# A linear-attention kernel: state carried on every 64 tokens instead of every 128

## What is computed

```python
qp, kp, v = phi(proj(Wq, bq)), phi(proj(Wk, bk)), proj(Wv, bv)   # phi = elu + 1
def step(carry, inp):
    kv, ksum = carry
    kt, vt, qt = inp
    kv = kv + einsum('bhd,bhe->bhde', kt, vt)
    ksum = ksum + kt
    num = einsum('bhd,bhde->bhe', qt, kv)
    den = einsum('bhd,bhd->bh', qt, ksum)[..., None] + EPS
    return (kv, ksum), num / den
...
x = x + out @ Wo.T + bo
```

## Time and profile before

| | |
|---|---|
| runs | 1939.35 us median of 3 (1937.93 to 1939.39) |
| profiled execution | 1939.27 us, span 1937.6 us |
| PE busy | 1904.0 us, 98% |
| VectorE busy | 1586.2 us, 82% |
| ScalarE busy | 664.3 us, 34% |
| POOL busy | 891.4 us, 46% |
| mean granted clock of PE | 0.997 |

### The profile page before, as it was taken

The page is one execution under the profiler, slowest core; times in us unless marked ns, Lnnn a source line. Parts: engine busy times, 40 slices in busy tenths (PEclk is TensorE's granted clock), DMA queues, the critical chain, the costliest instruction groups (busy, mean ns, idle before and its releaser), DMA issues. The chain is left out here.

```text
span 1937.6 us, 60626 instructions
## 1 busy us (share of the span) xinstructions
PE 1904.0 (98%) x25412; PEld 1671.4 (86%) x25412; DVE 1586.2 (82%) x3379; ACT 664.3 (34%) x1297; POOL 891.4 (46%) x979
## 2 busy tenths in 40 slices
PE   7999999999999999999999999999999999999997
PEld 6788888888888888888888888888888888888886
DVE  6878878887879888778878987887788897878787
ACT  4333333333333233333333333333332333323331
POOL 4355443455443554534554445545345544355422
PEclk9999999999999999999999999999999999999998
DMA  6343234433343432333423334323433334333222
GB/s 202 94 133 106 92 111 125 127 110 104 100 127 110 128 118 74 127 121 115 122 99 105 116 111 138 113 85 111 132 116 116 98 96 129 113 126 119 75 72 84
DMA packets 171202, 218.03 MB, mean 113 GB/s; under 512 B 24369, under 2 KB 85809, under 8 KB 170929
## 3 DMA queue, kind: packets, MB, share of 16 engines
q1 hardware_dynamic: 168528, 213.59, 34.7%
q10 hardware_dynamic: 2400, 0.55, 0.1%
HBM read 151.02 MB, written 63.04 MB: 110 GB/s over the span
## 5 line engine op out<-in xcount | busy, mean ns | idle before, releaser
L1258 POOL TENSOR_TENSOR k_sum<-k_sum,q_raw 128x512 f32<-128x512 f32 x128 | 165.0, 1290 | 556.2 <-DVE q_raw L933 556.2
L836 ACT ACTIVATE e_tmp<-ring,bias_n 128x512 f32<-128x512 f32 x256 | 176.1, 688 | 509.9 <-PE ring L651 506.8
L922 DVE TENSOR_TENSOR s_mask<-ring,causal 128x512 f32<-128x512 f32 x512 | 314.9, 678 | 0.0
L669 PE MATMUL ring<-wv_hi,xt_hi 128*128 128x260 f32 x1024 | 299.3, 292 | 0.0
L669 PE MATMUL ring<-wo_hi,o_hi 128*128 128x260 f32 x1024 | 287.8, 282 | 1.2 <-ACT o_hi L886 1.0
L669 PE MATMUL ring<-wv_lo,xt_hi 128*128 128x260 f32 x1024 | 288.8, 282 | 0.0
L669 PE MATMUL ring<-wv_hi,xt_lo 128*128 128x260 f32 x1024 | 288.8, 282 | 0.0
L669 PE MATMUL ring<-wo_lo,o_hi 128*128 128x260 f32 x1024 | 288.4, 282 | 0.0
L669 PE MATMUL ring<-wo_hi,o_lo 128*128 128x260 f32 x1024 | 287.3, 284 | 0.9 <-DVE o_lo L1170 0.9
L886 ACT ACTIVATE o_hi<-num_ps 128x512 fp32r<-128x512 f32 x128 | 76.4, 597 | 475.0 <-PE num_ps L750 474.9
L651 PE MATMUL ring<-xt_hi,wk_hi 128*128 128x512 f32 x512 | 207.9, 406 | 5.2 <-DVE xt_lo L998 3.2
(11 more groups left out here) (140 smaller groups left out, 4060.3 us busy)
## 6 DMA issues: line engine op xcount, KB each, us to landing
x_tok<-in_x SPq DMA_DIRECT2D x128, 256.0 KB, 3.7
res<-in_x SPq DMA_DIRECT2D x128, 256.0 KB, 2.8
out<-res SPq DMA_DIRECT2D x128, 256.0 KB, 2.1
x_in<-in_x_t SPq DMA_DIRECT2D x124, 256.0 KB, 4.6
keys_turned<-k_turned SPq DMA_DIRECT2D x112, 256.0 KB, 2.0
k_tok<-keys_turned SPq DMA_DIRECT2D x448, 64.0 KB, 2.0
x_rows<-moments_rows SPq DMA_DIRECT2D x31, 512.0 KB, 3.7
k_t<-in_wk_t SPq DMA_DIRECT2D x4, 256.0 KB, 8.3
```

What stands on the lines that cost most here:

```text
L669: mm = pe.matmul(bank[:, 0:HW], rows[a](k), w[b][:, k, h, :], start=n == 0, stop=n == 3 * KD - 1)
L836: act.activation(e_tmp[:, m], bank, ACT.Relu, bias=bias_n[:, m, g:g + 1], scale=-1.0).then_inc(phi_relu.handle, 1)
L922: dve.tensor_tensor(s_mask[:, j], ring[:, st.bank(u)].rearrange("p (g t) -> p g t", g=KD), repeat(causal, KD), ALU.mult).then_inc(free[st. ...
L1258: pool.tensor_tensor(k_sum[:, g], k_sum[:, g], q_raw[:, g], ALU.mult).then_inc(prod.handle, 1)
```

## The change

The unit of the carried state becomes 64 tokens (`HT = 64`), two halves s = 0 and 1 of a tile:

- The scores are formed only inside a half: for every head two products of 64 keys by 64 queries, on array tiles of 32 rows by 64 columns. 32 products instead of 16; a mask covers 256 elements per partition instead of 512.
- `from_tile` has 32 products, each over 64 keys and 64 queries, on array tiles of 64 rows by 32 columns. Products whose rows lie on one side of the array and whose place in `num` belongs to the other bank ("crossed" ones, half of them) go to a place of their own, `apart`. ScalarE copies `apart` to SBUF (`apart_kept`), and VectorE adds it into `num` (`join_halves`) before `o_hi`.
- `from_state` and `add_state` are called for each half: the early half (`early_half`, s = 0) of the next tile directly behind the output projection of this tile, the late half (`late_half`, s = 1) where the whole visit stood. For s = 0 too, VectorE sums the state (`sum_state`, behind the residual) and ScalarE keeps it (`keep_state`, at the top of the tile), before the late half can read it. Each half of the state has its own `kv_ps`.
- The last tile of a pair now needs keys as well, for its early half. In the last step keys are turned, sent and fetched a tile earlier.
- Two small constants more are set at the start.

The diff, cut to its core:

```diff
+HT = P // 2
-    KEY_TILES = [(b, c) for b in range(n_blocks) for c in range(TPB) if b % 2 == 0 or c < TPB - 1]
+    KEY_TILES = [(b, c) for b in range(n_blocks) for c in range(TPB)]
-    s_mask = sb("s_mask", [P, HPG, KD, P])
+    s_mask = sb("s_mask", [P, HPG, KD, HT])
-    causal = sb("causal", [P, P])
+    causal = sb("causal", [P, HT])
+    apart_kept = sb("apart_kept", [P, 2, P])
-    kv_ps = num_ps[:, 0, 2 * P:2 * P + KD * HD]
+    kv_ps = [num_ps[:, n, 2 * P:2 * P + KD * HD] for n in range(2)]
+    apart = num_ps[:, :, 3 * P:4 * P]
...
             for g in range(KD):
...
-                for j, u in enumerate(scores_of(c)):
-                    rows = slice(j * HD, (j + 1) * HD)
-                    mm = pe.matmul(ring[:, st.bank(u), g * P:(g + 1) * P], k_t[rows, par, g, t], q_div[rows, par, g, t],
-                                   start=True, stop=True, skip_group_check=True, tile_position=(j * HD, 0))
+                for s in range(2):
+                    t = slice(c * P + s * HT, c * P + (s + 1) * HT)
+                    for j, u in enumerate(scores_of(c)):
+                        rows = slice(j * HD, (j + 1) * HD)
+                        mm = pe.matmul(ring[s * HT:(s + 1) * HT, st.bank(u), g * HT:(g + 1) * HT],
+                                       k_t[rows, par, g, t], q_div[rows, par, g, t], start=True, stop=True,
+                                       skip_group_check=True, tile_position=(j * HD, s * HT))
...
+        def from_state(off, c, s):
+
+            n = kv_before(off, c, s)
+            if first_of_pair(off, c, s):
                 return
+            pe.wait_ge(kv_kept.handle, kv_kept.at(HPG * n))
+            begins = (0, 1) if s == 0 else (1,) if first_of_pair(off, c, 0) else ()
             for g, j in HEADS_OF_PASSES:
+                r = j // 2
+                rows, t = slice(r * HT, (r + 1) * HT), slice(c * P + s * HT, c * P + (s + 1) * HT)
+                out, col = num_at(g, j, s)
+                pe.matmul(out, kv_diag[rows, g, j * HD:(j + 1) * HD], q_div[rows, off % 2, g, t],
+                          start=r in begins and g < 2, stop=r != s, skip_group_check=True, tile_position=(r * HT, col))
+
+        def add_state(off, c, s):
+
+            if last_of_pair(off, c, s):
+                return
+            n = KEY_TILES.index((off, c))
+            pe.wait_ge(keys_in[n % 2].handle, 16 * HPG * (n // 2 + 1))
+            rows = slice(s * HT, (s + 1) * HT)
+            for g in range(KD):
+                for j in range(HPG):
+                    cols = slice((g * HPG + j) * HD, (g * HPG + j + 1) * HD)
+                    mm = pe.matmul(kv_ps[s][j * HD:(j + 1) * HD, g * HD:(g + 1) * HD], k_tok[rows, n % 2, j, g],
+                                   v_tok[rows, c, cols], start=first_of_pair(off, c, s) and g == 0, stop=True,
+                                   skip_group_check=True, tile_position=(s * HT, j * HD))
+            if s == 0:
+                mm.then_inc(kv_added.handle, 1)
...
+            for four in range(0, HEADS, HPG):
+                for s in range(2):
+                    rows = slice(s * HT, (s + 1) * HT)
+                    for g, j in HEADS_OF_PASSES[four:four + HPG]:
+                        head = (g * HPG + j) * HD
+                        out, col = num_at(g, j, s) if j // 2 == s else apart_at(g, j, s)
+                        mm = pe.matmul(out, v_tok[rows, c, head:head + HD], s_mask[rows, j, g], start=False, stop=True,
+                                       skip_group_check=True, tile_position=(s * HT, col))
+                    if four == HEADS - HPG:
+                        mm.then_inc(summed.handle, 1)
+
+        def early_half(st, off, c):
+
+            pe.wait_ge(o_lo.handle, o_lo.at(TPB * off + c))
...
+            from_state(off, c, 0)
+            add_state(off, c, 0)
+
+        def late_half(st, c):
...
+            from_state(st.off, c, 1)
+            add_state(st.off, c, 1)
+            from_tile(st, c)
...
                 if attn:
...
-                    from_state(st, c)
-                    add_state(st, c)
-                    from_tile(st, c)
+                    late_half(st, c)
...
                 if attn:
+                    if st.alone() and not last:
+                        early_half(st, st.off, c + 1)
...
                     two_halves(st, "O", c, [lambda k, h=h: o_t[h][:, k, :] for h in range(2)], w_o)
+                    if not st.alone():
+                        early_half(st, *tile_after(st.off, c))
...
+                if attn and not starts_late(st.off, c):
+                    keep_state(st.off, c, 0)
...
                 if attn:
-                    act.wait_ge(summed.handle, summed.at(st.lin(TPB, st.off, c + 1)))
+                    act.wait_ge(summed.handle, summed.at(2 * st.lin(TPB, st.off, c + 1)))
+                    act.activation(apart_kept, apart, ACT.Copy).then_inc(moved.handle, 1)
+                    act.wait_ge(joined.handle, joined.at(st.lin(TPB, st.off, c + 1)))
                     act.activation(o_wide[0], num, ACT.Copy).then_inc(o_hi.handle, 1)
...
+        def join_halves(st, c):
+
+            dve.wait_ge(moved.handle, moved.at(st.lin(TPB, st.off, c + 1)))
...
+            step = 2 * P * 2 - HT
+            sums = num_ps.rearrange("p n f -> p (n f)")[:, HT:HT + 2 * step].rearrange(
+                "p (n f) -> p n f", n=2)[:, :, 0:2 * P].rearrange("p n (g t) -> p n g t", t=P)[:, :, :, 0:HT]
+            rest = apart_kept.rearrange("p n (g t) -> p n g t", t=HT)[:, ::-1]
+            dve.tensor_tensor(sums, sums, rest, ALU.add).then_inc(joined.handle, 1)
...
                 if attn:
+                    join_halves(st, c)
                     dve.wait_ge(o_hi.handle, o_hi.at(st.lin(TPB, st.off, c + 1)))
                     dve.tensor_tensor(o_wide[1], num, o_wide[0].bitcast(F32), ALU.subtract).then_inc(o_lo.handle, 1)
-                    sum_state(st, c)
+                    sum_state(st.off, c, 1)
...
+                if st.alone() and not last:
+                    sum_state(st.off, c + 1, 0)
                 if attn:
                     residual(st, c)
+                    if proj:
+                        sum_state(*tile_after(st.off, c), 0)
```

More of the change, by code:

```diff
@@ L464, in run, with kv_before, first_of_pair, last_of_pair @@
         after_first()
-        body(Step(0, -1, ("proj", "turn"), base_m1))
+        st = Step(0, -1, ("proj", "turn"), base_m1)
+        body(st)
         for t in range(n_blocks - 2):
-            body(Step(0, t, ALL, base_at(t)))
+            st = Step(0, t, ALL, base_at(t), st)
+            body(st)
         t = n_blocks - 2
[L469 to L484, removed]
-        rows = (2 * (g % 2) + j % 2) * HD
-        return num_ps[rows:rows + HD, j // 2, g // 2 * P:(g // 2 + 1) * P], rows
+        st = Step(0, t, ("attn", "proj"), base_at(t), st)
+        body(st)
+        body(Step(0, t + 1, ("attn",), [a + b for a, b in zip(base_at(t), per_bank(("attn", "proj")))], st))
+    def kv_before(off, c, s):
+        return off // 2 * (4 * TPB - 1) + 2 * (TPB * (off % 2) + c) + s
+    def first_of_pair(off, c, s):
+        return off % 2 == 0 and c == 0 and s == 0
+    def last_of_pair(off, c, s):
+        return off % 2 == 1 and c == TPB - 1 and s == 1
+    def tile_after(off, c):
+        return (off, c + 1) if c < TPB - 1 else (off + 1, 0)
+    def starts_late(off, c):
+        return off == 0 and c == 0
+    def num_at(g, j, s):
+        rows = (2 * (g % 2) + j % 2) * HD
+        first = g // 2 * P + s * HT
+        return num_ps[rows:rows + HD, j // 2, first:first + HT], rows
+    def apart_at(g, j, s):
+        rows = (2 * (g % 2) + j % 2) * HD
+        return apart[rows:rows + HD, s, g // 2 * HT:(g // 2 + 1) * HT], rows
     def phi_index(kind, g):
@@ L727, in from_state @@
-        def from_state(st, c):
-            pe.wait_ge(o_lo.handle, o_lo.at(st.lin(TPB, st.off, c)))
-            if first_tile(st, c):
+                for s in range(2):
[5 more added lines that the diff above has]
+                                       skip_group_check=True, tile_position=(j * HD, s * HT))
+                        if g == KD - 1 and s == 1:
+                            mm.then_inc(full[st.bank(u)].handle, 1)
@@ L746, in from_tile @@
                     pe.wait_ge(free[BANK[u]].handle, st.before(BANK[u]) + CREDIT)
[L747 to L764, removed]
-                                   tile_position=(0, j * HD))
+            for four in range(0, HEADS, HPG):
+                for s in range(2):
+                    rows = slice(s * HT, (s + 1) * HT)
[6 more added lines that the diff above has]
+                        mm.then_inc(summed.handle, 1)
```

96 lines of the change are left out of this document (56 added, 40 removed).

## The result

The changed kernel takes 2194.56 us, the median of four runs (2191.72 to 2206.07), against 1939.37 (1937.93 to 1942.03): a ratio of 1.1325, with an interval from 1.1281 to 1.137. That is slower by 255 us, where 1943 was forecast, and far outside the range. The profiled execution took 2197.29 us.

A forecast was written before the change was run, and what follows sets the result against it. The prediction took PE, start to start, as the bound. PE's own sum -38, tile 3 +13, keys +12 and +7, last block +10 gave +4 us on 1939.27: forecast 1943 us, range 1915 to 1985.

The forecast's parts named there:

- What bounds the kernel: Whole kernel: PE, busy 1904 of 1937.6 us, longest wait 11.0 us, so the time is PE's, start to start.
- PE's own sum: On PE: late halves save 135 us, early halves cost 97 us, together -38 us.
- The late half: PE's attention visit in each tile: 1.90 us where a normal visit took 3.08, saving 135 us in all.
- The early half: PE's new visit behind the output projection: 0.81 us, or 0.56 without state, +97 us in all.
- The rival of dense starts: PE's visits: PE cannot keep up a start every 7 ns; at 11 ns +95 us, 2038 us; chance 0.10.
- Tile 3's chain: VectorE before tile 3's output projection: the longer chain makes PE wait 0.4 us in 31 blocks, +13 us.
- Keys: PE's early add waits for fetched keys: +12 us at the next block's tile 0, +7 us at tile 3.
- The last block: Attention alone, state through both halves: 8.7 us from tile to tile instead of 6.56, +10 us in all.
- the signs I had named for a wrong forecast: A visit over 2.2 us, VectorE gaps ahead of tile 3's join, or PE's waits on others under 15 us.
- the slower cases: Later chain 1970 us (0.17), dense starts 2038 (0.10), unchanged round cost 2092 (0.03), slower part of own range (0.17).

The follow-up runs named there:

- experiment 5: A kernel of PE work alone, bursts of 64 to 512 passes between covers of full matmuls, with and without loads; 128 passes took 1.38 us.
- the fed kernel: The changed kernel with the scores moved behind the next projection and VectorE reading the values first: 2080.57 us, ratio 1.0722; repeated at 2076.87 us.

## Why the prediction was wrong

- **What bounds the kernel** was read rightly: PE, from the first start to the last. But the argument that nobody keeps PE waiting, so its time is its starts, holds only as long as its instructions arrive, and the sum has no term for that, though the page before lists q8's 203 packets. This is the first step that failed: it went in at nothing and measured up to 189 us, 110 in gaps and up to 79 in the clock behind them. The second is PE's own sum, -38 forecast and +39 measured, 77 us (next two points). Together they are a little more than the miss of 252: the 79 is an upper bound, and the 13 us forecast at tile 3 did not come.
- **The late half**, 1.90 us, is 2.39. I priced a round of 64 columns at 0.058 between two measured rounds; from first to last start it is 0.079 for values (0.63 / 8) and 0.087 for scores (0.70 / 8), and the add's is 0.043, not 0.032. The handovers came out as forecast, 0.48 in all against 0.46. Taken start by start, this visit has eights at 6.6 ns a pass, as the earlier trace rows, only in its state and in the first half of its values and of its scores, just behind a handover; later starts of the add, the values and the scores come at 16 to 17 ns a pair, 8.3 a pass, and each of these three groups takes 0.15 from its last start to the next group's first. In the bursts of experiment 5 the mean is 10.7. I had taken the pace of the first eights for the steady one; why the later ones are slower, no run here shows. So this term was mis-sized: a saving of 135 us measured as 74.
- **The early half**, 0.81, is 0.94: +97 became +113.
- **The rival of dense starts**, 2038 us at 0.10, pointed the right way and had the wrong mechanism: it priced 11 ns a start everywhere, and that is about what the bursts show (10.7), but the larger cost comes in lumps of up to 4 us, where a packet ends more than some 140 passes into a visit. No case of mine ended above 2092. On the price of a start the Trainium skill speaks against this change, and the direction was right: the advice of TensorEngine Tiling, Instruction Overhead, against taking a tiling factor from a dimension that is small already. The 25 ns floor of the Trainium skill (TensorE: Matmul & The Clock Gate, "Wait — 56ns, not 53.3ns?") is not what was seen: 64 passes of scores start within 0.85 us, 13 ns apart.
- **Tile 3's chain**, forecast as a wait of 13 us: 0.7 on s_mask; the 2.8 on o_hi are in the last block. The parts of it were right. VectorE's mask took 412 ns (410 forecast), the join 420 (410). The 29.6 us of waits ahead of the join lie in tile 2 (25.5); tile 3 has 0.3:

```profile
L981 DVE TENSOR_TENSOR s_mask<-ring,causal 128x256 f32<-128x256 f32 x512 | 179.0, 412 | 20.7 <-PE ring L745 20.6
...
L1086 DVE TENSOR_TENSOR num_ps<-num_ps,apart_kept 128x256 f32<-128x256 f32 x112 | 47.0, 420 | 29.7 <-ACT apart_kept L943 29.6
```

  The chain had 0.4 us too little only against a PE that arrives 1.18 earlier. PE came 0.69 earlier at best, and later after a stall, so the slack stayed.
- **Keys**: forecast 12 + 7, measured 13.8: 11.7 for the next block's tile 0 in 16 blocks, right in place and size, and 2.0 for tile 3 in two. On the fed kernel, 30 to 33; PE comes sooner there, which is the likely reason and was not tried.
- **The last block**: forecast 8.7 us from tile to tile, measured 11.3, 12.6 and 11.2. The longest, in PE's timeline:

```profile
2148.34 0.46 PE L762 MATMUL num_ps<-q_div,kv_diag 64*32 64x64 f32 x32
...
2149.89 0.91 PE L745 MATMUL ring<-q_div,k_t 32*64 32x64 f32 x64
2154.50 0.83 PE L762 MATMUL num_ps<-q_div,kv_diag 64*32 64x64 f32 x30 [3.69 <-ACT kv_diag L909]
...
2160.98 0.46 PE L762 MATMUL num_ps<-q_div,kv_diag 64*32 64x64 f32 x32
```

  From the end of the values (about 2149.96) to the early half it is 4.5 us, where my steps of the state's chain sum to 3.8. What I left out is that the granted clock fell behind this wait, to 0.53 in the window after it (columns as above), and the output projection of 2.9 us in it takes 5.3. The three tiles take 35.2 us against 18.8 before, 16 more where 7 were forecast; a wait of 1.8 at the first late half (2 forecast) and 4.1 behind the last values (1 forecast) make it 22, of which 1.7 are a wait on issue that is counted above.

```profile
2155.00:2161.00 6.00, 6.00 (x79) 5.80 (x67) 0.79 (x3) 1.23 (x4) 1.28 (x1) 0.53 0.32 108
```
 
- Of the signs I had named for a wrong forecast, one came: a visit over 2.2 us. The sign that would have told the cause, waits on issue, I had not named. I had given the slower cases 0.47 in all, none of them by this mechanism.

## What to carry to other kernels

Count the instructions PE gets between two stretches of long matmuls, not only its columns: 256 (128 passes with their weight loads) ran without a stall here, at 320 a visit the kernel lost 1.3% and at 384 it lost 5%. If an edit multiplies short matmuls, place them between projections rather than side by side, and look at the page's instruction queue before and after. A gap of a few microseconds on a PE that is the bound has a second price, since the projection behind it may run at 1.2 GHz.

## What was not expected of the hardware

- PE's instructions come in packets of 16 KB, 256 instructions, each mostly 0.9 to 1.4 us on q8. A PE that is out of them stands for about 2 us, always at a packet's border. A starved PE advances by one packet in 3.5 to 4.3 us, with a median of 3.7 beside idle DMA engines and 4.0 beside loads of 170 GB/s.
- PE's stock always covered the 256 instructions of a 128-pass burst (16 of 16), and sometimes more: up to 271 passes, 542 instructions, ran ahead of a first gap.
- Whether a burst of 192 stalls depends on where the packets' border falls in it: the nine that did not stall had no border from 159 passes on, the seven that did had one at 143 (0.3 us idle) or at 159, 175 or 191.
